# Edge counts of a graph kernel: zeroing by one DMA, and all counting one-hots on VectorE twelve chunks ahead

## The reference

```python
edge_index = jnp.stack([src, dst])                       # 20625 edges
...
def _rgcn(x, edge_index, edge_type, weight, root, bias):
    msgs = x[src]
    out = x @ root + bias
    for r in range(weight.shape[0]):                     # 8 relations
        mask = (edge_type == r).astype(x.dtype)
        sums = jax.ops.segment_sum(msgs * mask[:, None], dst, num_segments=n)
        cnt = jax.ops.segment_sum(mask, dst, num_segments=n)
        mean = sums / jnp.maximum(cnt, 1.0)[:, None]
        out = out + mean @ weight[r]
```

## Time and profile before

| | |
|---|---|
| median of 3 runs | 1857.23 us |
| profiled execution, its own time | 1856.47 us |
| its span | 1854.8 us |
| busy: TensorE, VectorE, ScalarE, GpSimd | 1758.7, 999.0, 491.1, 711.3 us |
| DMA | 162.18 MB, mean 87 GB/s |

### The profile page before, as it was taken

One profiled execution on the slowest core, in us unless ns is written; L12 is line 12 of the kernel. 1 busy time (PEld: TensorE's weight loads), 2 busy tenths in 40 slices (PEclk: granted clock), 3 DMA queues, 4 the chain that ended last, 5 costly groups with the idle time before them and its releaser, 6 DMA issues.

```text
span 1854.8 us, 27729 instructions
## 1 busy us (share of the span) xinstructions
PE 1758.7 (95%) x9548; PEld 1440.6 (78%) x9548; DVE 999.0 (54%) x2478; ACT 491.1 (26%) x935; POOL 711.3 (38%) x613
## 2 busy tenths in 40 slices
PE   5999999999999999999999999855999999999999
PEld 4774688877787877777787877743899888879987
DVE  7997889985435262545435277777622224351311
ACT  3328788861101010111101154352100000111100
POOL 2100000024353536354353553200585552446862
PEclk9999999999999999999999999957999999999999
DMA  4432232233212213121223542110354351113322
GB/s 130 144 99 76 82 100 82 80 93 115 74 57 62 88 46 95 40 84 45 73 57 119 189 118 79 46 47 7 111 174 143 107 157 36 41 52 119 91 74 67
DMA packets 129654, 162.18 MB, mean 87 GB/s; under 512 B 14288, under 2 KB 75868, under 8 KB 129297
## 3 DMA queue, kind: packets, MB, share of 16 engines
q1 hardware_dynamic: 101743, 121.95, 22.2%
q10 hardware_dynamic: 21730, 22.51, 3.9%
q0 software_dynamic: 6080, 16.40, 2.9%
HBM read 135.51 MB, written 25.30 MB: 87 GB/s over the span
## 4 chain that ended last, share of the span: by engine, by line
PE 77%; DVE 12%; ACT 5%; issue 3%; DVEq 2%; DMA 1%; POOL 1%; ACTq 0%; SPq 0%
PE ps L371 20%; PE ps L372 20%; PE ps L373 19%; PE ps L1378 9%; DVE w_lo L322 1%; PE ps L1001 1%; ACT sc_code L921 1%; DVE adj L988 1%; PE ps L1343 1%; ACT counts L973 1%; DVE key_start L872 1%; PE ps L1298 1%; POOL w_lo L280 1%; DMA w_stage<-in_stream 1%; DMA nat<-in_x 1%
## 5 line engine op out<-in xcount | busy, mean ns | idle before, releaser
L371 PE MATMUL ps<-w_hi,xt_hi 128*125 128x512 f32 x1320 | 539.3, 409 | 12.4 <-DVE xt_lo L560 3.5
L260 POOL TENSOR_TENSOR w_hi<-w_stage,zero 128x512 fp32r<-128x512 f32 x258 | 277.8, 1077 | 678.7 <-PE ps L373 653.9
L372 PE MATMUL ps<-w_lo,xt_hi 128*125 128x512 f32 x1320 | 523.2, 396 | 0.0
L373 PE MATMUL ps<-w_hi,xt_lo 128*125 128x512 f32 x1320 | 521.9, 395 | 0.0
L263 POOL TENSOR_TENSOR w_lo<-w_stage,w_hi 128x512 fp32r<-128x512 f32 x258 | 351.1, 1361 | 20.2
L371 PEld LDWEIGHTS ps<-w_hi,xt_hi 128*125 128x125 f32 x1320 | 246.9, 187 | 71.0 <-DVE xt_lo L560 4.3
L373 PEld LDWEIGHTS ps<-w_hi,xt_lo 128*125 128x125 f32 x1320 | 246.1, 186 | 63.3
L372 PEld LDWEIGHTS ps<-w_lo,xt_hi 128*125 128x125 f32 x1320 | 246.6, 187 | 53.4
L371 PE MATMUL ps<-xt_hi,w_hi 128*128 128x314 f32 x736 | 241.0, 327 | 0.8 <-DVE ring L2584 0.7
L373 PE MATMUL ps<-xt_hi,w_lo 128*128 128x314 f32 x736 | 225.8, 307 | 0.0
L372 PE MATMUL ps<-xt_lo,w_hi 128*128 128x314 f32 x736 | 225.7, 307 | 0.0
(11 more groups left out here) (433 smaller groups left out, 2208.7 us busy)
## 6 DMA issues: line engine op xcount, KB each, us to landing
w_stage<-in_stream SPq DMA_DIRECT2D x374, 256.0 KB, 2.7
pre<-ring POOLq DMA_DIRECT2D x30, 250.0 KB, 4.2
a_qt<-pre_t SPq DMA_DIRECT2D x18, 312.5 KB, 3.8
a_qt<-pre_t ACTq DMA_DIRECT2D x14, 312.5 KB
pre_t<-ring_t POOLq DMA_DIRECT2D x12, 312.5 KB, 3.1
pre_t<-ring_t ACTq DMA_DIRECT2D x12, 312.5 KB
a_vx<-pre SPq DMA_DIRECT2D x9, 312.5 KB
nat<-pre SPq DMA_DIRECT2D x2, 1250.0 KB
```

Of the source, the lines that this page charges most:

```text
L260: POOL.tensor_tensor(w_hi[:, q, :], w_stage[:, q % NST, :], zero[:].to_broadcast([128, 512]), ALU.add).then_inc(S("hi_done"), 1)
L371: PE.matmul(dst, l_hi, r_hi, start=first, stop=False)
L372: PE.matmul(dst, l_hi, r_lo, start=False, stop=False)
L373: return PE.matmul(dst, l_lo, r_hi, start=False, stop=last)
```

## The change

The zeroing copies of ScalarE go. Instead ScalarE writes a run of 659 float zeros and issues one DMA that copies it 19 times into every partition of `adj` (12521 words), before step 0 of the scatter and behind the wait for `mk_ranked`. VectorE waits for that DMA ahead of `slot_keys`. `load_bias` and its place stay. In the counting, ScalarE's one-hots go and VectorE makes all of them, twelve chunks ahead, with 16 column and 4 row buffers; the row one-hot of a group of four chunks is made behind the addition of an even chunk, in the same gap as the register loads, and the low half moves behind it, ahead of the odd chunk's addition. Of the first twelve chunks' one-hots four come before and eight after the evacuation of group 5.

```diff
-    hot_col = [tmp(f"hot_col{i}", [128, SPLIT], F16, 1) for i in range(8)]
-    hot_row = [tmp(f"hot_row{i}", [128, 128, 4], F16, 1) for i in range(2)]
+    NHOT, NROWS = 16, 4
+    hot_col = [at(f"hot_col{i}", [128, SPLIT], F16, r_hot + i * 640) for i in range(NHOT)]
+    assert NHOT * 640 <= sc_per * 1248
+    hot_row = [tmp(f"hot_row{i}", [128, 128, 4], F16, 1) for i in range(NROWS)]
+    ZERO, ZERO_RUN = NBUCKET * NB // 2 + 1, 659
+    assert ZERO % ZERO_RUN == 0
+    zeros = tmp("zeros", [P, ZERO_RUN], F32, 1)
...
-    LEAD_HOT, STARTS = 6, 4
+    LEAD_HOT, STARTS = 12, 4
...
+    def hist_row(c):
+
+        if c >= 4 * NROWS:
+            DVE.wait_ge(S("hi_pe"), c - 4 * (NROWS - 1))
+        DVE.tensor_tensor(hot_row[c // 4 % NROWS][:], iota_by4[:],
+                          slot_row[:, c:c + 4].unsqueeze(1).to_broadcast([128, 128, 4]),
+                          ALU.is_equal)
+
     def hist_hot(c):
 
-        if c % 4 == 0:
-            if c >= 8:
-                DVE.wait_ge(S("hi_pe"), c - 4)
-            DVE.tensor_tensor(hot_row[c // 4 % 2][:], iota_by4[:],
-                              slot_row[:, c:c + 4].unsqueeze(1).to_broadcast([128, 128, 4]), ALU.is_equal)
-        if c % 6 == 5:
-            return
-        if c >= 8:
-            DVE.wait_ge(S("hi_pe"), c - 7)
-        DVE.tensor_scalar(hot_col[c % 8][:], col_key[:], slot_col[:, bass.ds(c, 1)], None,
+        if c >= NHOT:
+            DVE.wait_ge(S("hi_pe"), c - NHOT + 1)
+        DVE.tensor_scalar(hot_col[c % NHOT][:], col_key[:], slot_col[:, bass.ds(c, 1)], None,
                           ALU.is_equal).then_inc(S("hi_dve"), 1)
...
-            if c % 6 == 5:
-                PE.wait_ge(S("hi_act"), c // 6 * 2 + 2)
-            PE.wait_ge(S("hi_dve"), c + 1 - (c + 1) // 6)
+            PE.wait_ge(S("hi_dve"), c + 1)
...
+        wait(ALE, sig(ALE.activation(zeros[:], zero[0:P, :].to_broadcast([P, ZERO_RUN]), ACT.Copy), "act_step"))
+        wait(ALE, mk_ranked)
+        ALE.dma_start(adj[:].bitcast(F32).rearrange("p (n w) -> p n w", w=ZERO_RUN),
+                      zeros[:].unsqueeze(1).to_broadcast([P, ZERO // ZERO_RUN, ZERO_RUN])).then_inc(S("ld_bt"), 16)
...
             if s == 0:
                 evacuate_plain(SC0 - 1)
                 load_bias(SC0)
-                wait(ALE, mk_ranked)
-            if 1 <= s <= KT:
-                z0 = (s - 1) * zero_per
-                zn = min(zero_per, ZERO - z0)
-                t_ = ALE.activation(adj[:].bitcast(F32)[:, z0:z0 + zn], zero[0:P, :].to_broadcast([P, zn]), ACT.Copy)
-                if s == KT:
-                    mk_zero = sig(t_, "act_step")
...
-        wait(DVE, mk_zero)
+        DVE.wait_ge(S("ld_bt"), 32)
         DVE.wait_ge(S("sc_pe"), sc_per + EC + 1)
-        mk_slots = slot_keys()
-        for c in range(LEAD_HOT):
+        slot_keys()
+        for c in range(4):
+            if c == 0:
+                hist_row(c)
             hist_hot(c)
         evacuate(SC0 + 1)
+        for c in range(4, LEAD_HOT):
+            if c % 4 == 0:
+                hist_row(c)
+            hist_hot(c)
...
-        ALE.wait_ge(S("ld_bt"), 16)
-        wait(ALE, mk_slots)
-        hist_hot_act(5)
+        ALE.wait_ge(S("ld_bt"), 32)
         for h in range(HI_GROUPS):
             for n in range(per):
-                ahead = 2 * (h * per + n) + 1 + LEAD_HOT
-                if ahead % 6 == 5 and ahead < NCHUNK:
-                    hist_hot_act(ahead)
...
+                c = 2 * (h * per + n)
+                ahead = c + LEAD_HOT
+                hist_add(c, starts[c])
+                if ahead % 4 == 0 and ahead < NCHUNK:
+                    hist_row(ahead)
+                if ahead < NCHUNK:
+                    hist_hot(ahead)
+                if c % STARTS == 0 and c + STARTS < NCHUNK:
+                    starts.update(zip(range(c + STARTS, c + 2 * STARTS), hist_starts(c + STARTS)))
+                if chunk_at(h, n):
+                    split_dve(chunk_at(h, n))
+                hist_add(c + 1, starts[c + 1])
+                if ahead < NCHUNK:
+                    hist_hot(ahead + 1)
```

More of the change, by code:

```diff
@@ L708, in build @@
     slot_row = tmp("slot_row", [128, NCHUNK], F16, 1)
-    hot_col = [tmp(f"hot_col{i}", [128, SPLIT], F16, 1) for i in range(8)]
-    hot_row = [tmp(f"hot_row{i}", [128, 128, 4], F16, 1) for i in range(2)]
+    NHOT, NROWS = 16, 4
[5 more added lines that the diff above has]
+    zeros = tmp("zeros", [P, ZERO_RUN], F32, 1)
     zero16 = tmp("zero16", [P, NCHUNK], BF16, 1)
-    col_off = [tmp(f"col_off{i}", [128, SPLIT], F16, 1) for i in range(2)]
     slot_bits = tmp("slot_bits", [128, 2, NCHUNK], I32, 1)
@@ L935, in slot_keys @@
         DVE.tensor_copy(slot_row[:], slot_bits[:, 1, :])
-        return sig(DVE.drain(), "dve_step")
-    LEAD_HOT, STARTS = 6, 4
+        DVE.drain()
+    LEAD_HOT, STARTS = 12, 4
     def pair_bank(g):
         return 4 if g % 2 else 6
-    def hist_hot(c):
-        if c % 4 == 0:
-            if c >= 8:
-                DVE.wait_ge(S("hi_pe"), c - 4)
-            DVE.tensor_tensor(hot_row[c // 4 % 2][:], iota_by4[:],
-                              slot_row[:, c:c + 4].unsqueeze(1).to_broadcast([128, 128, 4]), ALU.is_equal)
-        if c % 6 == 5:
-            return
-        if c >= 8:
-            DVE.wait_ge(S("hi_pe"), c - 7)
-        DVE.tensor_scalar(hot_col[c % 8][:], col_key[:], slot_col[:, bass.ds(c, 1)], None,
-                          ALU.is_equal).then_inc(S("hi_dve"), 1)
[L958 to L965, removed]
+    def hist_row(c):
[4 more added lines that the diff above has]
+                          ALU.is_equal)
+    def hist_hot(c):
+        if c >= NHOT:
+            DVE.wait_ge(S("hi_pe"), c - NHOT + 1)
+        DVE.tensor_scalar(hot_col[c % NHOT][:], col_key[:], slot_col[:, bass.ds(c, 1)], None,
+                          ALU.is_equal).then_inc(S("hi_dve"), 1)
     def hist_copy(g):
@@ L997, in hist_pe @@
             c = 2 * g + j
-            if c % 6 == 5:
-                PE.wait_ge(S("hi_act"), c // 6 * 2 + 2)
-            PE.wait_ge(S("hi_dve"), c + 1 - (c + 1) // 6)
-            PE.matmul(ps[0:P, pair_bank(g) + j, 0:SPLIT], hot_row[c // 4 % 2][:, 0:P, c % 4], hot_col[c % 8][:],
+            PE.wait_ge(S("hi_dve"), c + 1)
+            PE.matmul(ps[0:P, pair_bank(g) + j, 0:SPLIT], hot_row[c // 4 % NROWS][:, 0:P, c % 4], hot_col[c % NHOT][:],
                       start=True, stop=True).then_inc(S("hi_pe"), 1)
@@ L1043, in beside @@
         SC_STEPS = -(-EC // sc_per)
-        ZERO = NBUCKET * NB // 2 + 1
-        zero_per = -(-ZERO // KT)
+        wait(ALE, sig(ALE.activation(zeros[:], zero[0:P, :].to_broadcast([P, ZERO_RUN]), ACT.Copy), "act_step"))
+        wait(ALE, mk_ranked)
+        ALE.dma_start(adj[:].bitcast(F32).rearrange("p (n w) -> p n w", w=ZERO_RUN),
+                      zeros[:].unsqueeze(1).to_broadcast([P, ZERO // ZERO_RUN, ZERO_RUN])).then_inc(S("ld_bt"), 16)
         def columns(s):
@@ L2588, in evac_turned @@
         if (g, b) == (1, 0):
-            DVE.wait_ge(S("ld_bt"), 32)
+            DVE.wait_ge(S("ld_bt"), 48)
         if g - 1 not in TURNED1:
```

## The result

The changed kernel takes 1894.43 us, the median of 4 runs (1892.04 to 1897.16), the kernel before on the same chip 1856.64 (1855.05 to 1858.44): ratio 1.0204, 95% interval 1.0186 to 1.0221. It is slower, as forecast, but by 38 us where the forecast had 20, and just beyond the range's upper end of 1893. The profiled execution took 1894.89 us, with a span of 1893.5.

What follows compares the result with a forecast made beforehand. The prediction took TensorE, busy 95%, as the bound, except where it waits for ScalarE in the scatter and VectorE's chain in counting. 1856.5 - 8.4 + 30.4 + 2 - 4.3 gave 1876 us, range 1863 to 1893.

Steps and rivals of the forecast that it cites:

- What bounds the kernel: Whole kernel: TensorE busy 95%; scatter paced by ScalarE while it zeroes, counting by VectorE's chain, 147 of 165.3 us.
- Part 1: Scatter: seven ScalarE zeroings go, steps take 4.88 instead of 6.08 us; -8.4 us.
- Part 3: Counting: all 40 column one-hots moved to VectorE fit gaps between additions; 0, otherwise +8.4 us.
- Part 4: Counting: order -3.8, fewer waits through more lead -2, more one-hots before the first addition +1.5; sum -4.3 us.
- Part 2: Zero DMA before scatter: holds ScalarE's next bias issue, so step 1 starts at 175.4, not 144.97; +30.4 us (+23 to +36).
- B: Rival at the zero DMA: no issue is held, the bias only queues; 1854 us, chance 0.09.
- C: Rival at the zero DMA: zeros go over all 16 engines and land by 153; 1844 us, chance 0.08.
- A2: Rival at the zero DMA: it holds ScalarE in its own issue, delaying step 0 too; 1884 us, chance 0.12.
- 130 GB/s: 48.2 us alone: Zero DMA: 6.26 MB on five engines at 130 GB/s would take 48.2 us without other traffic.
- other traffic: During the zero DMA: weights and ring stores on the same five engines add 6.5 us before the bias issue's release.
- Clock: Scatter after 32 us of TensorE idle: some 3.5 us at half clock; +2 us (0 to 4).

Runs made afterwards that it cites:

- count_only: Changed kernel without its zero DMA: ScalarE zeroes in eight pieces as before, the new counting stays; 1851.36 us, ratio 0.9974.
- dma_only: Kernel before with only its zeroing replaced by the run of zeros and the DMA (column buffers moved); 1898.41 us, ratio 1.0228.
- bias_first: Changed kernel with group 4's bias load issued ahead of the zero DMA instead of behind it; 1844.32 us, ratio 0.993.
- bias_late: Changed kernel with group 4's bias load behind step 4 of the scatter instead of behind step 0; 1873.19 us, ratio 1.0094.
- Experiment 8: Changed kernel with the run of zeros first stored to device memory and the zero DMA reading it from there; 1878.44 us, ratio 1.0117.
- split_bias: Changed kernel with zeros in two DMAs (partitions 112 to 124, then 0 to 111) and group 4's bias load ahead of them; 1843.48 us, ratio 0.9937.
- run_3584: Changed kernel with a run of 896 floats copied 14 times, packets of 3584 instead of 2636 bytes; 1880.4 us, ratio 1.0133.
- half_dma: Changed kernel with only 9 of 19 runs zeroed by DMA, ScalarE zeroing the rest behind steps 1 to 4; 1856.76 us, ratio 1.0007.
- split_112: Changed kernel with the zeros in two DMAs, partitions 112 to 124 first, then 0 to 111; 1852.55 us, ratio 0.998.

## Why the forecast was right in sign and wrong in size

*What bounds the kernel, Part 1 and Part 3* held. The zeroings' 8.4 us and the 1.5 us for more one-hots ahead of the first addition make -6.9; measured from step 1 to the first addition is -7.2. The forty column one-hots cost nothing: behind each lone addition there is room, as in VectorE's timeline after, where a one-hot stands in every gap and neighbouring additions are still 0.52 us apart:

```profile
340.85 0.32 DVE L984 TENSOR_TENSOR adj<-adj,counts 125x314 int16 x1
341.08 0.30 DVE L960 TENSOR_SCALAR hot_col<-col_key,slot_col 128x314 f16<-128x314 f16 x1
341.37 0.32 DVE L984 TENSOR_TENSOR adj<-adj,counts 125x314 int16 x1
```

*Part 4* was right and a little small. Without the one-hots ahead, the forecast for order and waits was -5.8; the additions' stretch shrank by 6.5. VectorE's waits for ScalarE's counts fell from 5.8 to 0.9 us, and 0.79 us is what a gap with a row one-hot and the four register loads takes. With the one-hots ahead, count_only gives -4.9 for a forecast of -4.3.

*Part 2 is the step that failed*, in one term. The mechanism was right: the bias issue is held, step 1 behind it, and TensorE with it; dma_only, bias_first and bias_late show it from three sides, and rivals B (1854) and C (1844) fell, as did A2, since the zero DMA's own issue took 1.46 us. The size was wrong: +30.4 was written, +50.6 came, beyond the upper bound of +36. The term "130 GB/s: 48.2 us alone" took its rate from the earlier trace rows, large transfers of 125 partitions between on-chip and device memory. The zero DMA reads and writes on-chip memory, and that ran at 85 GB/s on the same five engines. Experiment 8 changes the source, and then the rest of the sum is good: 130.7 to 175.2 in the prediction is 44.5 us from first data to release; there the first zero packet starts 0.9 us behind the issue, and to the release it is 44.7 us. The rest of 485 packets is 10.1 us at that rate (prediction 10.2), and other traffic is left with 5.5 us (44.7 less 1890 packets at 127 GB/s; prediction 6.5). In the changed kernel 38 + 6.5 us became 65. The terms don't come apart as well there: from the first zero packet at 130.90 to the release 2085 packets, 5.50 MB, moved at 85 GB/s with the other traffic already in it, since the first microseconds were faster; the rest of 290 packets is 9.0 us. The sum with 85 GB/s in place of 130 and the 10.2 and 6.5 us kept gives 70 us, 5 above the measured 65. So the rate is the term that failed, and with one rate of 85 for the whole copy nothing is left over for the traffic. The bounds failed with it. They varied the rate only from 129 to 131 GB/s, the spread of the rows at hand, and none of those rows was a copy of this kind; an operation that the trace doesn't show wanted bounds from further away.

The Trainium skill, DMA: Bandwidth & Descriptors, section "Issuing engines are not separate DMA queues", has the sequencer's time to initiate a DMA as usually small relative to the DMA. Here it is 52.2 us for a load that otherwise takes 0.53 to issue; the measurement decides against applying that rule to an issue behind a large one on its queue. The same page's rule on the number of engines (section "Why a DMA increments its semaphore by 16 and not by 1") gives 5 for 125 partitions and 16 for 112, and the traces agree: a share of 0.31 for 125, of 0.98 to 1.03 for 112 (other queues included).

*Clock*: +2 us was added, and nothing of it came. The granted clock is 0.50, the 1.2 GHz level, from 150 us to the end of the idle stretch and still after it, and from 202 us on it is 1.00 again:

```profile
198.00:200.00 2.00, 2.00 (x7) 1.22 (x7) 2.00 (x13) 1.77 (x5) 0.00 (x0) 0.50 0.54 179
200.00:205.00 5.00, 5.00 (x26) 3.36 (x24) 4.72 (x25) 4.47 (x14) 0.00 (x0) 0.86 0.33 84
```

but ScalarE's columns keep their distance of 4.88 us meanwhile (198.23, 203.11), and step 1 to the first addition is 81.97 us with some 6 us at the low level at its start, and 82.13 in split_bias (144.80 to 226.93) without an idle stretch ahead. The pace there is the hand-over between ScalarE and VectorE, and TensorE follows it even at half clock.

The terms as they came out: -1.0 before step 0, +51.6 of hold and late step, -7.2 scatter, -6.5 additions, +1.7 behind them: 38.6 for the 38.7 of the spans. The last lies within the spread of single runs (1855.05 to 1858.44) and isn't explained.

## What to carry to other kernels

Before a large DMA is put on an engine's queue, look for the next DMA that this engine issues: its compute waits with that issue until the large one is down to its last few hundred packets, 52 us here. The cure is order: issue small loads first, or leave the queue alone until the transfer is over (-50 us for one moved line); issues on SyncE's queue took 0.33 us beside the same transfer. Then ask for the number of partitions (112 filled 16 engines, 125 five) and price a copy by a row with the same source and destination, not by the rate of another kind of transfer; where there is none, keep the bounds wide.

## What the hardware showed that was not expected

- A copy within on-chip memory on five engines ran at 85, 87, 89 and 101 GB/s in four kernels (changed kernel, dma_only and run_3584 from 160 to 170 us; bias_late 1.01 MB from 175 to 185), with all five busy all the time, but at 113 (changed kernel, 133 to 138) and 117 (half_dma, 138 to 143) early on; from device memory it was 127, 127 and 133 with packets of 1792, 2636 and 7168 bytes. Packet size isn't it. Why the on-chip rate varies stays open.
- On five engines an issue is let go with 208 to 562 packets of the DMA ahead still to come, at sizes from 1792 to 7168 bytes: with 7168 bytes each that was 2.77 MB, and the hold was 24.8 us, against 37.4 with 1792 and with 2636 bytes from the same memory. Meanwhile issues on another queue are not held.
- Filling all 16 engines brought only 96 GB/s at a share of 0.98 in the first 8 us and 318 from 150 to 160 (split_112). In split_bias, where nothing is held, TensorE stayed busy beside it.
